# Attention on one core: the first tile of each round of the product with values is issued in two parts, and the next round waits for the first part

## The reference

```python
q = hidden_state @ Wq + bq;  k = encoder_hidden_state @ Wk + bk;  v = encoder_hidden_state @ Wv + bv
q = q.reshape(b, l, KVH, GROUPS, HD).transpose(0, 2, 3, 1, 4)      # 8 key heads, 4 query heads each, HD = 32
scores = jnp.einsum('bkgld,bksd->bkgls', q, k) * scale + mask
attn = jax.nn.softmax(scores, axis=-1)
out = jnp.einsum('bkgls,bksd->bkgld', attn, v)                     # the product with values
x = out.reshape(b, l, H) @ Wo + bo + hidden_state
return (x - mu) * jax.lax.rsqrt(var + EPS) * gamma + beta
```

## Time and profile before

| | |
|---|---|
| median of three runs | 1751.58 us |
| lowest, highest run | 1750.33, 1755.17 us |
| span of the profiled execution | 1749.3 us |
| mean granted clock of TensorE in it | 0.974 of full speed |
| PE busy | 1602.6 us, 92% of the span |
| DVE busy | 1448.7 us, 83% |
| ACT busy | 1385.7 us, 79% |
| POOL busy | 935.7 us, 53% |

### The profile page before, as it was taken

The page is one execution under the profiler, slowest core; times in us unless marked ns, Lnnn a source line. Parts: engine busy times, 40 slices in busy tenths (PEclk is TensorE's granted clock), DMA queues, the critical chain, the costliest instruction groups (busy, mean ns, idle before and its releaser), DMA issues. The chain is left out here.

```text
span 1749.3 us, 38438 instructions
## 1 busy us (share of the span) xinstructions
PE 1602.6 (92%) x14048; PEld 1110.0 (63%) x14048; DVE 1448.7 (83%) x2773; ACT 1385.7 (79%) x3186; POOL 935.7 (53%) x731
## 2 busy tenths in 40 slices
PE   3898879999899989999899998999989999999986
PEld 2665556576566765676576775667666676667654
DVE  4489878789788996889888898789988899788886
ACT  3578868769888787978889789787888878887794
POOL 5426433526754458534675448662585545856382
PEclk8999999999999999999999999999999999999998
DMA  9669987646885578664796567965678646875331
GB/s 178 186 148 227 241 232 199 182 135 168 250 257 144 138 187 286 188 154 122 209 288 185 130 175 192 287 178 127 174 238 252 158 133 170 292 208 150 84 114 67
DMA packets 357292, 325.02 MB, mean 186 GB/s; under 512 B 145776, under 2 KB 248176, under 8 KB 357104
## 3 DMA queue, kind: packets, MB, share of 16 engines
q1 hardware_dynamic: 357104, 322.56, 67.5%
HBM read 244.85 MB, written 83.89 MB: 188 GB/s over the span
## 5 line engine op out<-in xcount | busy, mean ns | idle before, releaser
L1941 PE MATMUL bank<-ring_hi,w_sb 128*128 128x512 f32 x2368 | 785.5, 399 | 32.1 <-issue 19.2
L1725 ACT ACTIVATE probs<-probs,shift 128x512 f32<-128x512 f32 x1024 | 726.9, 713 | 92.1 <-DVE shift L1826 91.0
L1839 DVE STREAM_TRANSPOSE turned_p<-probs 128x2048 f32<-128x2048 f32 x256 | 585.7, 2297 | 154.3 <-PE bank L2021 149.3
L1826 DVE CUSTOM_DVE_ANT_0 probs<-bank,mask_l 128x512 f32<-128x512 f32 x1024 | 643.1, 680 | 56.3 <-PE bank L2001 37.2
L1626 POOL TENSOR_TENSOR w_sb<-w_raw,w_sb 128x512 fp32r<-128x512 f32 x320 | 412.1, 1297 | 413.8 <-ACT w_sb L1682 413.7
L1941 PEld LDWEIGHTS bank<-ring_hi,w_sb 128*128 128x128 f32 x2368 | 444.4, 189 | 149.9 <-issue 42.6
L1941 PE MATMUL bank<-ring_lo,w_sb 128*128 128x512 f32 x1184 | 467.9, 395 | 0.0
L2001 PE MATMUL bank<-k_stack,q_stack 96*128 96x512 f32 x1024 | 358.9, 414 | 12.7 <-DVE shift L1826 10.0
L2021 PE MATMUL bank<-turned_p,v_all 32*32 32x512 f32 x8192 | 307.9, 642 | 65.8 <-DVE turned_p L1839 48.6
L1638 POOL TENSOR_TENSOR ring_lo<-x_t,ring_hi 128x512 fp32r<-128x512 f32 x168 | 214.7, 1291 | 144.9 <-ACT ring_hi L1694 144.4
L2001 PEld LDWEIGHTS bank<-k_stack,q_stack 96*128 96x128 f32 x1024 | 186.1, 189 | 143.3 <-issue 62.9
(11 more groups left out here) (75 smaller groups left out, 933.2 us busy)
## 6 DMA issues: line engine op xcount, KB each, us to landing
w_raw<-w_d SPq DMA_DIRECT2D x144, 256.0 KB, 3.7
q_stack<-q_hi_d SPq DMA_DIRECT2D x128, 256.0 KB, 4.3
w_raw<-in_L_xattn_Wo_dram SPq DMA_DIRECT2D x128, 256.0 KB, 3.0
q_hi_d<-part_hi SPq DMA_DIRECT2D x64, 256.0 KB, 3.9
q_lo_d<-part SPq DMA_DIRECT2D x64, 256.0 KB, 5.0
q_stack<-q_lo_d SPq DMA_DIRECT2D x64, 256.0 KB, 3.9
v_all<-v_d SPq DMA_DIRECT2D x256, 64.0 KB, 2.2
out_dram<-y_sb SPq DMA_DIRECT2D x32, 512.0 KB, 3.0
```

The lines of the kernel that those rows point to most:

```text
L1725: nc.scalar.activation(probs[:, st % 2, h, :], probs[:, st % 2, h, :], ACT.Exp, scale=-1.0, bias=shift[:, g % 2, i:i + 1], accum_out=sums[ ...
L1826: nc.vector.tensor_tensor_reduce(out=probs[:, st % 2, h, :], in0=S_ps[h][:, :], in1=mask_l[:, st, :], scale=-1.0, scalar=HIGHEST, op0=ALU. ...
L1839: nc.vector.transpose(turned_p[:, :, :, st, :].rearrange("p j h c -> p h j c"), probs[:, st % 2, :, :].rearrange("p h (j c) -> p h j c", c ...
L1941: mm = nc.tensor.matmul(C[c][:, :], w_sb[:, n_w, (1, 0, 0)[third], d % 4, :], (hi, lo, hi)[third], start=(n == 0), stop=(n == 23))
```

## The change

The 512 columns of the first tile (c, r) = (0, 0) of rounds 0, 1 and 2 are issued as two matmuls: heads 0 to 2 (384 columns) at their old place, with an increment of a new semaphore `pv_round`, and head 3 (128 columns) after the other 15 tiles of the round. The first instruction of rounds 1, 2 and 3 waits for the increment of the round before. The last round and the other 15 tiles are as they were. `start` is set on the first part only.

```diff
-        pv_done, pv_out = sem("pv_done"), sem("pv_out")
+        pv_round, pv_done, pv_out = sem("pv_round"), sem("pv_done"), sem("pv_out")
...
+            def pv_tile(g, jj, c, r, h0, h1):
+                j = 4 * jj + c
+                return nc.tensor.matmul(PV_ps[r][32 * c:32 * (c + 1), P * h0:P * h1],
+                                        v_all[32 * r:32 * (r + 1), g % 2, HD * j:HD * (j + 1)],
+                                        turned_p[32 * r:32 * (r + 1), j, h0:h1, :, :].rearrange("p h a c -> p (h a c)"),
+                                        start=(jj == 0 and h0 == 0), stop=(jj == 3), skip_group_check=True)
...
-                    for jj in range(4 * n // PV_PARTS, 4 * (n + 1) // PV_PARTS):
-                        for c in range(4):
-                            for r in range(4):
-                                j = 4 * jj + c
-                                mm = nc.tensor.matmul(...)
-                    if n == PV_PARTS - 1:
-                        mm.then_inc(pv_done, 1)
+                    for jj in range(4):
+                        if jj > 0:
+                            pe.wait_ge(pv_round, 3 * G + jj)
+                        for c, r in itertools.product(range(4), range(4)):
+                            if (c, r) == (0, 0) and jj < 3:
+                                pv_tile(g, jj, c, r, 0, 3).then_inc(pv_round, 1)
+                            else:
+                                mm = pv_tile(g, jj, c, r, 0, 4)
+                        if jj < 3:
+                            pv_tile(g, jj, 0, 0, 3, 4)
+                    mm.then_inc(pv_done, 1)
```

More of the change, by code:

```diff
@@ L1 @@
+import itertools
 from contextlib import ExitStack
```

## The result

| | before | changed |
|---|---|---|
| median | 1750.8 us (1750.0 to 1755.2, 6 runs) | 1759.7 us (1753.2 to 1764.7, 6 runs) |
| span of the profiled execution | 1749.3 us | 1757.6 us |
| warm product, first to last matmul start | 3.87 us | 3.91 us |

The ratio is 1.0048, with a 95% interval of 1.0034 to 1.0061: 0.5% slower, where +3 us and "within 0.3%" had been forecast. The median of the kernel before is the one measured beside the changed kernel.

A forecast was written before the change was run, and what follows sets the result against it. TensorE's matmul stream was taken to bound the kernel, the product held by a full queue. Added instructions cost 3.2 us, wait, part two and increments nothing: +3 us, 1751.6 + 3 = 1754.6 us, range 1740 to 1773.

The forecast's parts named there:

- The full queue: In the product, TensorE holds at most 64 instructions, oldest first, so rounds follow at 1.07 us though passes stream in 0.86.
- The wait costs nothing: At round changes, the wait is over at 0.85 us, before the full queue admits tile 1's load at 1.08: no cost.
- part two nothing: Head 3 on tile 0: it is free at 0.94 us, ahead of tile 1's load at 1.08, so no cost.
- the increment nothing: The three pv_round increments a product cost nothing inside TensorE's stream; the skill's 26 ns each was not charged.
- Rival A: Round changes: the stall is a busy tile's load price that the wait avoids; 42 us faster, 0.19 with weaker forms.
- Rival B: Round changes: a waiting load holds until everything ahead has ended; 21 us slower, 1773 us, chance 0.09.
- C: Rival: nothing measurable, the extra 0.05 us a product lies under waits for turns; 1751.6 us, chance 0.12.
- Added instructions: Product's round changes: 12 instructions more a product, 768 in all, make each change 0.017 us later, 3.2 us in all.
- a sum of small costs: Slower case: small costs, increments among them, add up to over 5 us; chance 0.05.

The follow-up runs named there:

- half_rounds: Kernel before with each product's 64 matmuls reordered: four rounds of tiles c = 0, 1, then four of c = 2, 3; 1881.1 us, one run.
- wait_only: Kernel before with the first tile left whole, its matmul incrementing pv_round and the next round waiting for it; 1759.2 us, ratio 1.0041.
- split_four: Changed kernel with the first tile of rounds 0 to 2 in four one-head parts, without wait or increments; 1792.4 us, 1.0231 to the kernel before.
- split_only: Changed kernel without the pv_round increments and waits, first tile still in two parts; 1760.4 us, 1.0043 to the kernel before.
- b_shift60: Kernel before with 15 small matmuls (60 instructions) added at TensorE's idle start, products untouched; 1749.3 us, ratio 0.9978.
- b_shift32: Kernel before with 8 small matmuls (32 instructions) added at TensorE's idle start, products untouched; 1778.4 us, ratio 1.0146.

## Why the prediction was right and wrong

- *The full queue.* Right for this change. Warm products went from 3.87 to 3.91 us, 3.0 us in all, for 3.2 predicted: a round change cost 0.015 us where 0.017 was charged. half_rounds shows that a busy tile alone doesn't hold loads back, wait_only that a wait doesn't free them. split_four shows that the count isn't the whole rule.
- *The wait costs nothing, part two nothing, the increment nothing.* Right: with and without wait and increments the kernel takes the same (1.0048 and 1.0043). Three increments a product at the figure of the Trainium skill would have been 5.0 us, an estimate (page "TensorE: Matmul & The Clock Gate", section "The cost: per-tile semaphore tail"); inside a stream the traces show none of it: a warm product takes 3.91 us with the increments and without.
- *Rival A* fell with wait_only and half_rounds. *Rival B* fell with the rounds at 1.07 us, where it had 1.21, and with split_only. *C* is out: the products' total is longer by 8.2 us, and TensorE's wait for turns is 48.6 us as before, so nothing was hidden under it.
- *The step that failed* is "Added instructions", or what it left out: the 768 instructions were priced only for their place among the 64 held, and not for having to be fetched. They shift every later instruction against the blocks of 256, by 12 more with each product, and they make a product, 256 instructions before, 268 long. With the products' phases drawn anew, four stalls took the place of one: +6.2 us. I had left a chance of 0.05 for "a sum of small costs" and 0.14 for slower in all, without knowing of a mechanism that moves this kernel by -4 to +25 us (b_shift60, b_shift32). How much of the loss is the change's own can't be read from one placement of the blocks: the three that were tried gave 1.0048, 1.0074 and 1.0039, and none gained. The row that could have warned me stands in the earlier trace rows: product 57's stall of 1.9 us was in the trace of before, hidden in the means.
- The time, 1759.7, lies in the range by luck. It is over the 1757 that the forecast's own range went up to, and the range reached on to 1773 only for rival B, which fell.

## What to carry to other kernels

Count the instructions. 64 small matmuls as two-pass tiles are 256 instructions, a whole fetched block in 4 us, so a dense burst of small matmuls can outrun its own instruction stream; look for idle "issue" time in front of a matmul that waits for no semaphore. And when an edit adds or removes instructions on a busy engine, a change of 1% can come from where the blocks fall (here up to 1.5%, with the products untouched): before a small gain or loss is believed, run the kernel with a few dozen idle instructions at its start.

## What was not expected of the hardware

- TensorE's instructions come in DMA packets of 16 KB, 256 instructions. Inside the products a missing block held it for up to 3.8 us, at instruction 193 or 194 of the block before in every stall of over 0.5 us, and it went on 1.2 to 1.6 us after the packet's end. What the packet's start waits for wasn't found.
- After such a stall the granted clock was 0.50 for 3.2 us or more behind product 31 of b_shift32, and for 10 us behind product 23 of the changed kernel.
- 32 instructions more at the start of a kernel of 28,644, in idle time, made it 1.5% slower.
- A tile of TensorE that is busy costs nothing by itself: with 8 tiles of 32x32 in turn each pass follows at 0.43 us. With 16 tiles a round of two passes takes 1.07 in the changed kernel instead of 0.86, which fits 64 held instructions that are just about one round.
